# A sandwich block whose middle sum is transposed without its norm

## The reference

```
x1  = x  + LN(Attention(LN(x)))          # 16 heads, rotary, causal softmax, output projection y = o @ Wo
out = x1 + LN(FFN(LN(x1)))
FFN(h): scores = 8 * softmax(h @ Wr.T + br)      # 8 experts
        low    = h @ A.T                          # 8 experts x rank 16 = 128 columns
        e      = 2 * sum over experts of (low * scores) @ B
LN(v) = (v - mean(v)) / sqrt(var(v) + 1e-5), over the 1024 columns
```

## Time and profile before

| | |
|---|---|
| time, median of 3 runs | 1081.9 us |
| the profiled execution's own time | 1081.56 us |
| its span, first to last instruction | 1079.7 us |
| mean granted TensorE clock | 0.997 |
| busy: TensorE, VectorE, ScalarE, GpSimdE | 1059.9, 739.4, 626.6, 435.4 us |
| last y matmul of tile 15 starts | 1053.74 us |

### The profile page before, as it was taken

How to read it: one execution, slowest core, us unless ns; L and a number is a source line. 1 busy time by engine, 2 the same in 40 slices (tenths; PEclk the granted TensorE clock), 3 DMA queues, 4 the chain that set the end, 5 groups by cost and what they waited for, 6 DMA issues and landing times.

```text
span 1079.7 us, 20016 instructions
## 1 busy us (share of the span) xinstructions
PE 1059.9 (98%) x5566; PEld 887.4 (82%) x5566; DVE 739.4 (68%) x2025; ACT 626.6 (58%) x1437; POOL 435.4 (40%) x417
## 2 busy tenths in 40 slices
PE   7999999999999999999999999999998999999996
PEld 6888888888888888888888888888886888888885
DVE  8777777776666666666666666666666777677776
ACT  6566666666555655555565655555575554555444
POOL 4153343435262544435253534445365222332222
PEclk9999999999999999999999999999999999999998
DMA  7122324242211346111010202021232223322311
GB/s 277 36 83 70 126 69 131 68 131 75 82 51 29 108 166 225 22 64 49 29 53 29 68 10 68 10 72 49 92 124 56 84 97 118 113 82 97 117 59 59
DMA packets 58517, 90.34 MB, mean 84 GB/s; under 512 B 3552, under 2 KB 36320, under 8 KB 58464
## 3 DMA queue, kind: packets, MB, share of 16 engines
q1 hardware_dynamic: 58320, 89.44, 25.3%
q10 hardware_dynamic: 144, 0.26, 0.1%
HBM read 64.52 MB, written 25.17 MB: 83 GB/s over the span
## 4 chain that ended last, share of the span: by engine, by line
PE 92%; DVE 3%; issue 1%; ACT 1%; POOL 1%; DVEq 0%; ACTq 0%; POOLq 0%
PE bank L1412 50%; PE bank L1343 30%; PE bank L1439 6%; PE bank L1564 2%; PE bank L1549 1%; PE bank L1385 1%; PE bank L1565 1%; PE bank L1373 1%; DVE stats L1263 0%; POOL big_lo L621 0%; PE bank L1355 0%; DVE k_lo L1071 0%; PE bank L1594 0%; POOL w_lo L626 0%; DVE prob L1033 0%
## 5 line engine op out<-in xcount | busy, mean ns | idle before, releaser
L1412 PE MATMUL bank<-big_hi,w_hi 128*128 128x512 f32 (+1 forms) x776 | 331.9, 428 | 0.3 <-DVE big_lo L1014 0.3
L571 POOL TENSOR_SCALAR prob<-prob,rinv 128x128 f32<-128x128 f32 (+3 forms) x256 | 149.0, 582 | 447.3 <-DVE rinv L1043 447.3
L706 ACT ACTIVATE prob<-prob,nmax 128x128 f32<-128x128 f32 (+3 forms) x256 | 143.9, 562 | 312.4 <-DVE nmax L1033 311.2
L1412 PE MATMUL bank<-big_hi,w_lo 128*128 128x512 f32 (+1 forms) x776 | 305.5, 394 | 0.0
L1412 PE MATMUL bank<-big_lo,w_hi 128*128 128x512 f32 (+1 forms) x776 | 303.7, 391 | 0.0
L1412 PEld LDWEIGHTS bank<-big_hi,w_lo 128*128 128x128 f32 x776 | 145.8, 188 | 32.2
L1051 DVE TENSOR_TENSOR pT_lo<-bank,pT_hi 128x128 fp32r<-128x128 f32 (+3 forms) x256 | 123.6, 483 | 56.9 <-ACT pT_hi L717 54.3
L1412 PEld LDWEIGHTS bank<-big_hi,w_hi 128*128 128x128 f32 x776 | 147.1, 190 | 17.0 <-issue 0.4
L1412 PEld LDWEIGHTS bank<-big_lo,w_hi 128*128 128x128 f32 x776 | 147.7, 190 | 11.9
L1033 DVE CUSTOM_DVE_ANT_0 prob<-bank,mask 128x128 f32<-128x128 f32 (+3 forms) x256 | 124.4, 486 | 21.8 <-PE bank L1343 16.9
L1043 DVE RECIPROCAL rinv<-rsum 128x1 f32<-128x1 f32 x256 | 40.8, 160 | 127.3 <-ACT prob L706 126.9
(11 more groups left out here) (134 smaller groups left out, 1924.2 us busy)
## 6 DMA issues: line engine op xcount, KB each, us to landing
w_raw<-in_wqkv SPq DMA_DIRECT2D x48, 512.0 KB, 4.2
attention_out<-o_sum SPq DMA_DIRECT2D x64, 128.0 KB, 2.3
w_raw<-attention_out SPq DMA_DIRECT2D x16, 512.0 KB, 4.7
land<-in_x SPq DMA_DIRECT2D x16, 512.0 KB, 3.6
out<-res SPq DMA_DIRECT2D x15, 512.0 KB, 2.6
xin<-in_x SPq DMA_DIRECT2D x12, 512.0 KB, 5.4
xT_hold_hi<-xin SPq DMA_DIRECT2D x8, 512.0 KB, 3.6
xT_hold_lo<-xn SPq DMA_DIRECT2D x8, 512.0 KB, 5.4
```

The lines of the kernel that those rows point to most:

```text
L571: pool.tensor_scalar(p, p, rinv[:, q % 4:q % 4 + 1], 1.0, ALU.mult, ALU.mult).then_inc(prob_done, 1)
L706: act.activation(prob[:, q % 4, 0:n], prob[:, q % 4, 0:n], ACT.Exp, scale=-1.0, bias=nmax[:, q % 4:q % 4 + 1], accum_out=rsum[:, q % 4:q % ...
L1412: done = pe.matmul(grp_ps[(b + k) % 2][:, cols], w, xt[:, cols], start=at == 0, stop=at == GROUP_MM - 1)
```

## The change

A layer norm does not change when a constant is added to all columns of a row. So the first norm's shift is not applied to make x1: the new x1 buffer holds x + y * rs1, and its missing shift nm1 is kept (two columns, one for each of two tiles). VectorE makes it straight from y's two banks with one fused instruction for each half (`x1_half_sum`). ScalarE's `y_normal` and `x1_normal`, and the buffers z and xn2, go. TensorE transposes x1 itself, without its norm, one tile earlier in the turns (`x2_turn(t - 1)`, behind `experts(t - 2)`; tile 0's stands in `y_half(1, 1, 1)`). The second norm is applied to the low-rank product: low = rs2 * (x1 @ [A; Wr].T) + nm2 * (column sums of [A; Wr].T) + br, with `low_base` for the last two terms. The column sums are made once: VectorE sums `ar_raw` over its eight chunks (`ar_sum`, a reduction with an inner step of 136 elements), TensorE multiplies by a matrix of ones (`columns`), VectorE copies the result. At the end of a tile, the third norm's shift nm3 and nm1 are added (`e_scale`), so that `mixture` applies both. In the diff the indentation is cut by eight columns and blank lines are left out; semaphore and buffer declarations, renamed calls (`ln_scale` to `x_scale` in the attention stage) and ScalarE's and SP's tails are not shown. SP stores tile 14 in two halves instead of one.

```diff
     def mixed(t, i):
-        pool.wait_ge(normed, normed_by(ln_third(t)))
+        pool.wait_ge(normed, mixed_by(t))
         pool.tensor_tensor(res[:, i, :], res[:, i, :], x1[:, i, :], ALU.add).then_inc(res_done, 1)
     def turn(t, i):
-        if late(t, 3):
-            mixed(t - 3, 1 - i)
         if not final(t):
             oT_low(t + 1, 1 - i)
+        mixed(t - 2, i)
     for t in range(2, 6):
         turn(t, t % 2)
...
         turn(t + 1, 1)
     for t in range(TILES - 2, TILES):
         turn(t, t % 2)
-    pool.wait_ge(last_z, 1)
-    pool.wait_ge(xres_in[1], 16 * TILES // 2)
-    pool.tensor_tensor(x1_last[:, half(0)], z[:, half(0)], xres[:, 1, half(0)], ALU.add).then_inc(x1_done, 1)
-    mixed(TILES - 3, 1)
-    mixed(TILES - 2, 0)
+    pool.wait_ge(before_norm, 1)
+    pool.tensor_tensor(res[:, 0, half(0)], res[:, 0, half(0)], x1[:, 0, half(0)], ALU.add).then_inc(before_add, 1)
+    pool.wait_ge(normed, mixed_by(TILES - 2))
+    pool.tensor_tensor(res[:, 0, half(1)], res[:, 0, half(1)], x1[:, 0, half(1)], ALU.add).then_inc(res_done, 1)
 @block.scalar
...
         act.wait_ge(wlt_done, t + 1)
         if late(t, 1):
             act.wait_ge(e_done, t)
-        act.activation(wlT_hi[:, :], o_ps[:, WLT:WLT + P], ACT.Copy).then_inc(wlT_hi_done, 1)
+        act.activation(wlT_hi[:, :], turned_low(t), ACT.Copy).then_inc(wlT_hi_done, 1)
     def turn(t, i):
-        x2T_high(t - 2, 0)
-        if late(t, 3):
-            mixture(t - 3, 1 - i)
-        x2T_high(t - 2, 1)
         ln_start(ln_first(t - 1))
         if not final(t):
             oT_high(t + 1, 1 - i, 8 * (t + i) + 16)
-        y_normal(t - 1, 1 - i)
         logits_exp(t - 2)
+        ln_start(ln_second(t - 1))
         wlT_high(t - 2)
-        ln_start(ln_second(t - 1))
-        x1_normal(t - 1, 1 - i)
+        x2T_high(t - 1, 0)
         ln_start(ln_third(t - 2))
+        x2T_high(t - 1, 1)
+        mixture(t - 2, i)
+    x2T_high(0, 0)
+    x2T_high(0, 1)
     for t in range(2, 6):
         turn(t, t % 2)
...
                     y_variance(0, 0)
                 if s == 3:
                     dve.memset(br_sb[:, 0:HR], 0.0).then_inc(br_zeroed, 1)
-                    ln_scale(ln_first(0))
-                    x1_sum(0, 0)
-                    dve.wait_ge(x1_done, 1)
-                    layernorm(ln_second(0), [x1[:, 0, 0:512], x1[:, 0, 512:1024]])
+                    dve.memset(ones[:, :], 1.0).then_inc(ar_sum_done, 1)
+                    y_scale(0, 0)
+                    x1_half_sum(0, 0, 0)
+                    x1_half_sum(0, 0, 1)
+                    x1_stats(0, 0, 0)
+                    x1_stats(0, 0, 1)
+                    ln_variance(ln_second(0))
                     o_add(u - 2, 1)
+                    x1_scale(0)
                     dve.wait_ge(ffn_hi_done, 1)
                     dve.tensor_tensor(ar_lo, ar_raw[:, :, :], ar_hi.bitcast(F32), ALU.subtract
                                       ).then_inc(ffn_lo_done, 1)
-    def x1_sum(t, i):
-        dve.wait_ge(normed, normed_by(ln_first(t)))
-        dve.wait_ge(xres_in[i], 8 * (t - i) + 16)
-        if late(t, 2):
-            dve.wait_ge(res_done, t - 1)
-        dve.tensor_tensor(x1[:, i, :], z, xres[:, i, :], ALU.add).then_inc(x1_done, 1)
+                    dve.tensor_reduce(ar_sum[:, :], ar_raw[:, :, :].rearrange("p c n -> p n c"), AX.X, ALU.add
+                                      ).then_inc(ar_sum_done, 1)
+    def half_stats(k, src):
+        dve.bn_stats(stats[:, k, :], src).then_inc(ln_stat, 1)
+    def y_scale(t, i):
+        ln_scale(ln_first(t), rs1, nm1[:, i:i + 1])
+    def x1_half_sum(t, i, k):
+        if k == 0:
+            dve.wait_ge(ln_dve, LN_STEPS * (ln_first(t) + 1))
+            dve.wait_ge(xres_in[i], 8 * (t - i) + 16)
+            if late(t, 2) and not final(t):
+                dve.wait_ge(res_done, t - 1)
+        dve.scalar_tensor_tensor(out=x1_of(t, i)[:, half(k)], in0=y_ps[i][k][:, :], scalar=rs1[:, 0:1],
+                                 in1=xres[:, i, half(k)], op0=ALU.mult, op1=ALU.add
+                                 ).then_inc((x1_half, x1_done)[k], 1)
+    def x1_stats(t, i, k):
+        dve.wait_ge((x1_half, x1_done)[k], t + 1)
+        half_stats(k, x1_of(t, i)[:, half(k)])
+    def x1_scale(t):
+        ln_scale(ln_second(t), rs2, nm2)
+    def low_base(t):
+        dve.wait_ge(ln_dve, LN_STEPS * (ln_second(t) + 1))
+        dve.scalar_tensor_tensor(out=base[:, :], in0=col_sum[:, :], scalar=nm2[:, 0:1], in1=br_sb[:, :],
+                                 op0=ALU.mult, op1=ALU.add).then_inc(base_done, 1)
     def y_variance(t, i):
         dve.wait_ge(y_done, t + 1)
...
     run_slots(dve, slot)
-    def e_stats(t):
-        dve.wait_ge(e_done, t + 1)
-        ln_stats([e_bank(t, k)[:, :] for k in range(2)])
-        ln_variance(ln_third(t))
+    def e_stats(t, k):
+        dve.wait_ge((e0_done, e_done)[k], t + 1)
+        half_stats(k, e_bank(t, k)[:, :])
+    def e_scale(t, i):
+        over, bias = (rstd_last, nmr_last) if final(t) else (rstd, nmr)
+        ln_scale(ln_third(t), over, nm3, None if final(t) else mixed_by(t - 1))
+        dve.wait_ge(ln_dve, LN_STEPS * (ln_third(t) + 1))
+        dve.tensor_tensor(bias[:, :], nm3[:, :], nm1[:, i:i + 1], ALU.add).then_inc(shifted, 1)
     def low_sum(t):
         m = 5 * t
         dve.wait_ge(low_done, t + 1)
-        if isinstance(t, int) and t == 0:
-            dve.wait_ge(br_zeroed, 1)
-            dve.wait_ge(ffn_in, 32)
-        dve.tensor_tensor(low_lo[:, :], o_ps[:, ARW:2 * ARW], br_sb[:, :], ALU.add).then_inc(soft_dve, 1)
+        dve.wait_ge(base_done, t + 1)
+        dve.scalar_tensor_tensor(out=low_lo[:, :], in0=o_ps[:, ARW:2 * ARW], scalar=rs2[:, 0:1], in1=base[:, :],
+                                 op0=ALU.mult, op1=ALU.add).then_inc(soft_dve, 1)
         dve.wait_ge(soft_dve, m + 1)
-        dve.tensor_tensor(low[:, :], o_ps[:, 0:ARW], low_lo[:, :], ALU.add).then_inc(soft_dve, 1)
+        dve.scalar_tensor_tensor(out=low[:, :], in0=o_ps[:, 0:ARW], scalar=rs2[:, 0:1], in1=low_lo[:, :],
+                                 op0=ALU.mult, op1=ALU.add).then_inc(soft_dve, 1)
         dve.wait_ge(soft_dve, m + 2)
         dve.tensor_reduce(lmax[:, :], low[:, HR:ARW], AX.X, ALU.max, negate=True).then_inc(soft_dve, 1)
...
                           x2T_hi[:, 4 * k:4 * k + 4, :].bitcast(F32), ALU.subtract).then_inc(x2T_lo_done, 1)
-    def half_stats(k, src):
-        dve.bn_stats(stats[:, k, :], src).then_inc(ln_stat, 1)
     def turn(t, i):
         dve.wait_ge(y_done, t)
-        half_stats(0, y_ps[1 - i][0][:, :])
-        if late(t, 3):
-            ln_scale(ln_third(t - 3))
-        x2T_low(t - 2, 0)
         half_stats(1, y_ps[1 - i][1][:, :])
         ln_variance(ln_first(t - 1))
-        x2T_low(t - 2, 1)
-        ln_scale(ln_first(t - 1))
+        low_base(t - 2)
+        y_scale(t - 1, 1 - i)
+        x1_half_sum(t - 1, 1 - i, 0)
         low_sum(t - 2)
-        x1_sum(t - 1, 1 - i)
+        x1_half_sum(t - 1, 1 - i, 1)
         weigh(t - 2)
-        dve.wait_ge(x1_done, t)
-        half_stats(0, x1[:, 1 - i, half(0)])
-        half_stats(1, x1[:, 1 - i, half(1)])
+        x1_stats(t - 1, 1 - i, 0)
+        x1_stats(t - 1, 1 - i, 1)
+        ln_variance(ln_second(t - 1))
         wlT_low(t - 2)
-        ln_variance(ln_second(t - 1))
-        ln_scale(ln_second(t - 1))
-        e_stats(t - 2)
+        x1_scale(t - 1)
+        e_stats(t - 2, 0)
+        e_stats(t - 2, 1)
+        ln_variance(ln_third(t - 2))
+        x2T_low(t - 1, 0)
+        e_scale(t - 2, i)
+        x2T_low(t - 1, 1)
+        dve.wait_ge(y0_done, t)
+        half_stats(0, y_ps[i][0][:, :])
+    dve.wait_ge(col_done, 1)
+    dve.tensor_copy(col_sum[:, :], tr_ps[:, 0:ARW]).then_inc(col_read, 1)
+    dve.wait_ge(ffn_in, 32)
+    dve.wait_ge(br_zeroed, 1)
+    dve.wait_ge(col_read, 1)
+    x2T_low(0, 0)
+    x2T_low(0, 1)
+    dve.wait_ge(y0_done, 1)
+    half_stats(0, y_ps[1][0][:, :])
...
         turn(t, t % 2)
     last, before = TILES - 1, TILES - 2
-    dve.wait_ge(last_y, 1)
-    half_stats(0, y_ps[1][0][:, :])
-    ln_scale(ln_third(TILES - 3))
     dve.wait_ge(y_done, TILES)
     half_stats(1, y_ps[1][1][:, :])
     ln_variance(ln_first(last))
-    x2T_low(before, 0)
-    ln_scale(ln_first(last))
-    dve.wait_ge(xres_in[1], 16 * TILES // 2)
-    scaled_sum(x1_last[:, half(1)], y_ps[1][1], xres[:, 1, half(1)], ln_first(last), rstd_last)
-    x2T_low(before, 1)
-    dve.wait_ge(normed, normed_by(ln_first(last)))
-    half_stats(1, x1_last[:, half(1)])
-    dve.wait_ge(x1_done, TILES)
-    half_stats(0, x1_last[:, half(0)])
+    low_base(before)
+    y_scale(last, 1)
+    x1_half_sum(last, 1, 0)
+    x1_half_sum(last, 1, 1)
+    low_sum(before)
+    x1_stats(last, 1, 0)
+    x2T_low(last, 0)
+    x1_stats(last, 1, 1)
     ln_variance(ln_second(last))
-    low_sum(before)
-    ln_scale(ln_second(last))
+    x2T_low(last, 1)
+    x1_scale(last)
+    low_base(last)
     weigh(before)
```

(96 more changed lines are left out.)

147 lines of the change are left out of this document (66 added, 81 removed).

## The result

The changed kernel takes **1094.45 us** (median of 4 runs, 1094.02 to 1094.62) against 1081.95 (4 runs, 1081.64 to 1082.09) of the kernel before: ratio 1.0116, 95% interval 1.0104 to 1.0128. It is slower by 12.5 us. The forecast was 1088.0, range 1084.3 to 1091.0: the direction was right, the size was half of it, and the time lies above the range.

A forecast was written before the change was run, and what follows sets the result against it. TensorE, busy 98% of the span, was taken as the bound. Shift of the last y matmul 6.0 + clock 1.4 - tail 1.15 = +6.25 us on 1081.56 gives 1087.8; forecast for the median 1088.0, range 1084.3 to 1091.0.

The forecast's parts named there:

- turns 2 to 15: In these turns TensorE's instruction count sets the time; the reordered VectorE and ScalarE chain to `wlT_low` costs 0 us.
- B: Turns 2 to 15: chain to `wlT_low` or GpSimdE's `mixed` takes 0.7 us more than counted; +4.9, 1093; chance 0.12.
- The spare of 0.35: In each turn, `wlT_low` would be ready with 0.35 us left before `experts` on TensorE wants it.
- The first stall: Stage start: TensorE waits 4.25 us before `columns()` for VectorE's reduction, taken as 1.25 us long.
- Rival E: Start: the reduction takes 2.5 us because its inner step is 136 elements; +1.2 on the forecast, 1089.2; chance 0.08.
- The clock: Start: the granted clock falls to half speed after the 4.25 us stall, costing 1.4 us.
- Rival A: Start: the 4.25 us stall comes without the clock's fall; +4.85 us, 1086.7; chance 0.14.
- The second wait: Start: `x2T_turn`-stage transposes of tile 0's second half wait for the first half's copy and subtraction; 1.0 us.
- The two blocks of transposes: TensorE has one more block pair of transposes before the last y matmul's end; 0.7 us.
- The tail: Behind the last y matmul: tile 15's stats start earlier; 1.15 us saved, 24.4 us to the span's end.
- Rival D: Tail: all of low_sum(15)'s 3.6 us lead arrives; 2.4 us more saved, 1085.6; chance 0.12.
- Rival C: Start: tile 0's sums are ready when TensorE asks, so no change; 1082.5; chance 0.09 together with anything faster.

The follow-up runs named there:

- `mixed` cut: Changed kernel with GpSimdE's add of x1 covering only 8 of 1024 columns in tiles 0 to 13; 1088.31 us (one run).
- the run with the stall filled: Changed kernel with twenty 512-column matmuls that nobody reads put into TensorE's stall before the columns matmul; 1092.86 us (one run).
- the best version: Changed kernel with `base` behind x1's scale, `wlT_hi` ahead of Ln and Exp, column sums by GpSimdE additions, start reordered; 1079.59 us, 0.9976 of the kernel before.

## Why the prediction was wrong

**The step that failed** is the one on turns 2 to 15: "So 0 us, covered by 0.35 us; each 0.1 us beyond costs 14 times that." It measured +6.10. The chain was the right one, and the rival that names it, B, gives 1093, the nearest of all to 1094.45; but B had 0.12, and its cause was not known. Against B it was said that all durations but the fused sums' were those of like turns. `base` is new as well, had no row, and is missing from the count of the turn (the tail's count has it, with 0.3); it seemed to fit under ScalarE's Ln and Exp, which it does at 0.35 us. I had reckoned GpSimdE's `mixed` as something that x1 waits for (2.41 us, done at 2.55, just in time), not as something that slows VectorE's own instructions while it runs. `base` takes 0.92 to 1.33 us there instead of 0.35, of which 0.24 had been left of Ln and Exp's time (turn 2, where `base` is quick, has that much idle behind it).

The spare of 0.35 was right outside the hardware loop and wrong in it. Counted from the turn's first `low_rank` product, x1's first half starts at 2.05 to 2.08 in a turn outside the loop when `base` is quick (`mixed` cut) and at 2.69 to 2.71 when it is slow: 0.63 late. To spare were some 0.38 (`wlT_lo` ended 0.45 to 0.50 ahead of `experts`; when TensorE waits for it there it is 0.10), and the turn is 0.3 longer. In the loop it starts at 2.35 even with the quick `base`, partly behind 0.2 us in which VectorE is idle in front of it and for which the profile names only VectorE's own last instruction. That had used up the spare and is the 0.12 a turn; the slow `base` adds 0.5 (2.86), and the turn is 0.66 longer. The prediction counted one kind of turn only. Its own sign of being wrong, turns longer than 15.33 us, came true. Taking away the meeting, from either side, gives back 6.1 and 6.7 us; taking away only its way to TensorE gives back 7.1. With `wlT_hi` ahead, in three kernels, the turns 2 to 15 take 214.64 to 214.81 us, 0.7 to 0.85 less than before, where -0.3 had been foretold.

The Trainium skill has the rule, and I did not apply it: "SBUF — State Buffer", section "Who interferes with whom", says that a VectorE instruction with two inputs in SBUF contends with a GpSimdE instruction that reads SBUF, and its section "SBUF: two separate sides" says that whichever starts first holds the shared ports for its whole length and the other blocks. The trace agrees: `base` reads `col_sum` and `br_sb`, starts second and ends 0.15 to 0.17 us behind `mixed`; `low_lo`, of the same size with one input in PSUM, stays at 0.35 beside a GpSimdE instruction that reads SBUF. What is left behind the end of `mixed` is shorter than the 0.35 of a `base` alone, so part of its time had passed by then; no run here shows the other order, VectorE first.

**The mis-sized terms** of the start, +9.15 against 7.65. The prediction counts from start to start, and so do the figures here; the 4.67 and 0.91 of the timelines are idle times, 0.17 less each.
- The first stall: 4.84 (833.93, where the next chunk would have started, to 838.77) against 4.25. The reduction took 2.08 where 1.25 was taken, and 1.28 with a step of 1 element. Rival E's mechanism, at two thirds of its size, and the side for which the Trainium skill, "SBUF — State Buffer", Specifications, was cited; the trace agrees with the direction, and the page gives no size. VectorE came to the reduction 1.57 us earlier than reckoned (836.63, not 838.2) and TensorE asked 1.31 earlier. Most of both is the attention stage's shift, which moves the two alike and cancels; the 0.26 left are the second memset, which cost nothing, and x1's chain, which ran with less between its steps: 4.25 + 0.83 - 0.26 = 4.82.
- The clock: 1.9 against 1.4, by the run with the stall filled; 1.4 in the two kernels where it fell at 838.5. That it would fall was right, and it fell also behind 3.85 us. Rival A is out.
- The second wait: 1.07 at full clock (idle 0.91), 1.0 foretold. The columns' matmul, 0.25 there behind the wait (0.14 and 0.15 in the two kernels in which it follows without one), 0.3 foretold.
- The two blocks of transposes with the matmuls' restarts behind each wait: 1.07, where 0.7 was taken for the blocks and nothing for the restarts. The start of 12.87 us at full clock, less the 5.51 of before, is 7.36, and that is 4.97 (the reduction took 2.21 in that run) + 1.07 + 0.25 + 1.07.

**The tail** came out right, 24.55 us against 24.4, -1.02 against -1.15, but partly by luck: `base` costs 0.95 more in it, which was not foretold. In the kernels with a quick `base` it is 23.8 to 24.0, so the hand-over of tile 14 was reckoned 0.4 to 0.6 too long, and the two nearly cancel. Rival D (2.4 more) is out. Rival C's mechanism, sums that are ready when TensorE asks, is what the version with the new start brings about: its start is 1.2 us longer than before, not 9.15, which is no more than the two blocks of transposes and the columns' matmul themselves.

Two figures of the prediction are slightly off, and neither matters: the earlier trace rows give 1.50 us from `low_turn` to `experts`, not 1.45, and 1087.81 with the 0.34 between 1081.56 and 1081.9 is 1088.15, not 1088.0.

**Not foretold**: -1.33 us in a stage whose work is not changed. It is no part of the change's idea, and the kernel before has it for five unused tiles. Measured against that kernel (1079.91), the best version (1079.59) wins 0.3 us. Each against the runs of the kernel before that were timed with it, the two are 2.0 and 2.6 us less, with ratios of 0.9981 and 0.9976 whose intervals overlap. By stretches the best version's start is 1.2 us longer than that kernel's, its turns 0.2 and its tail 1.6 shorter. So the idea shows no gain clear of the noise, and most of what the best version wins over the kernel before is had by five unused tiles too.

## What to carry to other kernels

Before adding an instruction to an engine, ask what its neighbours do in the same microsecond, not only whether it fits in a gap: two SBUF operands on VectorE beside an addition on GpSimdE cost 136 elements up to 1.33 us instead of 0.36. When a chain is nearly late, look for an in-order queue in which its next link stands behind work that needs the delayed part; swapping two lines there gave back 7.1 of 12.5 us and left the cause of the delay in place. And a wait at the head of an in-order queue's long list moves to the next consumer if one item is moved; it goes when the list itself is shared out.

## What the runs showed of the hardware

- `base` ended 0.15 to 0.17 us behind the end of GpSimdE's addition in all 14 turns, whether it had started 1.2 or 1.6 us after it (1.33 to 0.92 us long). An instruction of the same size with one operand in PSUM took 0.35 us beside GpSimdE.
- A reduction over 128x1088 fp32 took 2.08 to 2.25 us with an inner step of 136 elements and 1.28 with a step of 1.
- The granted clock stayed 1.00 for three us of TensorE's idleness behind 834.1 and fell between 837 and 838. Where the stall ended earlier (reduction of 1.28 us, TensorE at work again from 837.90), it fell all the same, at about 838.5, under running matmuls. A stall that ends before the clock has fallen is not yet without its price. With the same idle time of 4.67 us it fell anywhere between 836.0 and 839.0 in five kernels, and with TensorE at work again from 838.7 to 838.9 it was back between 841.5 and 844.5; their starts took 14.12 to 14.66 us, and 12.87 without the fall.
- 24 bytes a partition of unused tiles took 2.0 us (0.19%) off a kernel of 1082 us. A difference of 0.2% between two kernels whose tiles lie differently says nothing on the edit between them.
